# A three-block "macaron" kernel: feed-forward attention and its tail as one stage, distance tables written in parts, semaphores cleared a stage later

## What is computed

```
x = x + 0.5 * FFN(LN(x))
x = x + causal_attention(LN(x))        # 16 heads of 16, T = 1024, 32 relative distance buckets
x = x + 0.5 * FFN(LN(x))

FFN(x):                                # L = 8, N = 1024
  y1 = ln(x + mha(x), ln1)             # 4 heads; for each of 1024 positions over the L = 8
  gates = softmax(y1 @ wg); idx = argmax(gates)        # 8 experts
  loc = number of earlier tokens with the same idx; keep = loc < 1024
  h = y1 @ w1[idx] + b1[idx]           # 256 -> 1024, no nonlinearity
  z = h @ w2[idx] + b2[idx]            # 1024 -> 256
  y2 = ln(y1 + where(keep, gate * z, 0), ln2)
```

## Time and profile before

| | us |
| --- | --- |
| median of three runs | 2865.24 |
| runs | 2863.83, 2865.24, 2867.42 |
| the profiled execution's own time | 2867.24 |
| its span, first to last instruction | 2865.5 |

### The profile page before, as it was taken

One profiled execution on the slowest core, in us unless ns is written; L12 is line 12 of the kernel. 1 busy time (PEld: TensorE's weight loads), 2 busy tenths in 40 slices (PEclk: granted clock), 3 DMA queues, 4 the chain that ended last, 5 costly groups with the idle time before them and its releaser, 6 DMA issues. The chain is left out here.

```text
span 2865.5 us, 47996 instructions
## 1 busy us (share of the span) xinstructions
PE 2344.7 (82%) x15862; PEld 1425.3 (50%) x15864; DVE 2147.0 (75%) x5653; ACT 1658.5 (58%) x3995; POOL 820.4 (29%) x853
## 2 busy tenths in 40 slices
PE   3999998567739959999999999999869999983264
PEld 2666666456525523444444444444646666662243
DVE  3788888634859868898988988897447888876076
ACT  1545444313724427999999999999315445442154
POOL 1244343053544440000000000000113344331745
PEclk6999999778969978999999999999989999996587
DMA  8122120474225564454545455452341121111711
GB/s 170 30 67 67 45 67 30 162 251 138 73 88 173 170 150 89 97 111 93 109 95 113 92 103 103 99 109 45 119 154 52 45 67 54 58 38 62 210 63 68
DMA packets 244679, 281.50 MB, mean 98 GB/s; under 512 B 41808, under 2 KB 212880, under 8 KB 243808
## 3 DMA queue, kind: packets, MB, share of 16 engines
q1 hardware_dynamic: 218192, 218.81, 30.5%
q0 software_dynamic: 16384, 50.35, 5.6%
q10 hardware_dynamic: 9872, 9.45, 1.0%
HBM read 190.63 MB, written 94.16 MB: 99 GB/s over the span
## 5 line engine op out<-in xcount | busy, mean ns | idle before, releaser
L2146 DVE CUSTOM_DVE_ANT_0 banks<-banks,attn_bias 128x128 f32<-128x128 f32 (+7 forms) x1024 | 760.0, 778 | 108.4 <-PE banks L1855 82.6
L2059 ACT ACTIVATE attn_probT<-banks 128x512 f32<-128x512 f32 x1152 | 622.5, 621 | 61.6 <-PE banks L1872 51.3
L1855 PE MATMUL banks<-attn_kst,attn_qst 96*128 96x512 bf16 (+3 forms) x1536 | 421.6, 336 | 23.1 <-DMA attn_kst<-kparts 12.5
L1872 PE MATMUL banks<-attn_qst,attn_kst 99*128 99x256 bf16 (+3 forms) x2176 | 410.8, 281 | 15.2 <-ACT attn_probT L2059 7.1
L1894 PE MATMUL banks<-attn_probT,attn_vb 128*32 128x256 f32 (+3 forms) x4352 | 315.6, 400 | 7.7 <-ACT attn_probT L2059 7.2
L1872 PEld LDWEIGHTS banks<-attn_qst,attn_kst 99*128 99x128 bf16 x2176 | 187.5, 97 | 169.1 <-ACT attn_probT L2059 54.9
L2204 POOL CAST attn_lowp<-attn_lowT 128x32 bf16<-128x32 f32 x64 | 13.4, 209 | 852.3 <-DVE attn_lowT L2154 852.3
L420 PE MATMUL banks<-ffn_a_xT,winT 128*128 128x512 f32 x512 | 250.6, 612 | 6.0 <-ACT ffn_a_kT L621 2.9
L1855 PEld LDWEIGHTS banks<-attn_kst,attn_qst 96*128 96x128 bf16 x1536 | 117.4, 97 | 256.7 <-DVE attn_low L2146 158.6
L2047 ACT COPY banks<-attn_biasT 128x512 f32<-128x512 f32 x384 | 227.7, 628 | 29.9 <-DMA attn_biasT<-neardT 23.2
L883 POOL TENSOR_TENSOR ffn_a_xres<-ffn_a_xin,row_ffn_out 128x1024 f32<-128x1024 f32 x32 | 75.5, 2359 | 412.4 <-DVE ffn_a_res L764 387.2
(11 more groups left out here) (254 smaller groups left out, 4482.8 us busy)
## 6 DMA issues: line engine op xcount, KB each, us to landing
attn_qst<-qparts SPq DMA_DIRECT2D x384, 64.0 KB, 2.8
attn_kst<-kparts SPq DMA_DIRECT2D x192, 128.0 KB, 4.9
rows<-ffn_a_xb SPq DMA_DIRECT2D x32, 512.0 KB, 2.9
rows<-ffn_a_y SPq DMA_DIRECT2D x32, 512.0 KB, 3.1
ffn_t_xs<-in_L_ffn_w_dram SPq DMA_DIRECT2D x16, 1024.0 KB, 10.1
attn_biasT<-neardT SPq DMA_DIRECT2D x128, 128.0 KB, 5.1
attn_bias<-neard SPq DMA_DIRECT2D x128, 128.0 KB, 2.2
qparts<-qkv_part SPq DMA_DIRECT2D x32, 384.0 KB, 2.8
```

The costliest lines, as they stand in the source:

```text
L1855: mm = nc.tensor.matmul(score[k % 2][:, a:e], qst[0:K6, u, half, hh, ii * P:(ii + 1) * P], kst[0:K6, u, hh, a:e], start=True, stop=True)
L1872: mm = nc.tensor.matmul(tbank[t % 3][:, at:at + nb * P], kst[:, u, hh, j * P:(j + 1) * P], qst[:, u, half, hh, x:x + nb * P], start=(k == ...
L2059: nc.scalar.activation(probT[:, g % 2, i, 0:w], tbank[t % 3][:, 0:w], ACT.Exp, scale=-1.0).then_inc(s_exp, 1)
L2146: nc.vector.tensor_tensor_reduce(out=part, in0=part, in1=bias[:, hh, T - w:T], scale=1.0, scalar=BIG, op0=ALU.add, op1=ALU.min, accum_out= ...
```

## The change

The change has five parts.

1. **One stage for attention and tail.** `ffn_attention` no longer opens a stage: it returns five functions, one for each engine, which the tail's engine programs call first. Its tiles are slices that the tail lends it (`Lent`): `xin`, `xb`, `xres`, `qT`, `prob`, `res` and others from the first 7 parts of `flat`, `y1` from the eighth, `kT` from `w12`, `xT` from `xT`, `vv` from `y1` of the tail. Where the tail would write what attention still reads, an engine waits: `over_yet` for the last logits (TensorE in turn 0, VectorE, SyncE in turn 1), `stored` for the stores to `rows` (VectorE ahead of the one-hot chunks, GpSimd ahead of the gathers).
2. **Early loads.** In attention's last group SyncE issues W1[0], W1[1], W2[0] to W2[3] and b2 (turn 0) or b12 (turn 1).
3. **Order in the tail of turn 0.** TensorE: `turn_w1(0)`, `(1)` ahead of `counts`; `product(1)` and `turn_w1(3)` ahead of `inverse`; `bias_sum` one expert later; the first group's transposes ahead of the last two `bias_sum` and the marks. ScalarE: `scaled` in two pieces around `w12_out(1)` and `turned(3)`; `place(0, 0)`, `place(1, 1)` ahead of the last `w12_out`; `xT_out(0, 0)` ahead of the seeds.
4. **Tables in parts.** The two transfers in `prepare` become eight of four heads each, issued by SyncE in the first feed-forward attention in groups 2 to 9, behind that group's other transfers. `attention_core` waits for all eight.
5. **Clearing a stage later.** At a stage's end only the block's own join is left. The semaphores of a stage are cleared by GpSimd inside the next one (`clear_past`), behind its first work; those of the last stage not at all.

```diff
 class Phase
     def block(self):
-        self.callback(self._clear)
+        self.callback(self._pass)
         return self.enter_context(self.core.nc.Block())
-    def _clear(self):
-        for sem in self.sems:
-            self.core.nc.gpsimd.sem_clear(sem)
-        self.core.nc.all_engine_barrier()
+    def clear_past(self):
+        if self.core.past:
+            for sem in self.core.past.sems:
+                self.core.nc.gpsimd.sem_clear(sem)
...
 prepare, SyncE
-            for way, dst in enumerate((neard, neardT)):
-                src = bass.AP(tensor=relrow.tensor, offset=way * 3 * P, ap=[[2 * 3 * P, AH], [0, P], [1, 3 * P]])
-                sp.dma_start(bass.AP(tensor=dst.tensor, offset=1, ap=[[P * PITCH, AH], [PITCH + 1, P], [1, 3 * P]]),
-                             src).then_inc(core.tables, 16)
...
 ffn_attention, SyncE
             if not under(n, 4):
                 store(n - 4, u)
+            if n == NG - 1:
+                early_loads(sp)
+            if first and 2 <= n < 2 + len(tables):
+                sp.dma_start(*tables[n - 2]).then_inc(core.tables, 16)
...
+    def over_yet(eng):
+        eng.wait_ge(s_lgsb, NG)
+    def stored(eng, u):
+        eng.wait_ge(s_store[u], 16 * (NG // 2))
+        eng.wait_ge(s_ahead[u], 16 * (NG // 2))
...
 tail, now ffn
+        def early_loads(sp):
+            if turn == 0:
+                for e in range(2):
+                    load_w1(sp, e)
+                for e in range(4):
+                    load_w2(sp, e)
+                sp.dma_start(b12[:, :], row_bcast(d["L0_ffn_b2"].rearrange("e c -> (e c)"), NE * C)).then_inc(s_w, 16)
+            else:
+                sp.dma_start(b12[:, :], b12d).then_inc(s_w, 16)
...
 ScalarE
-                scaled()
-                for e in range(1, NE):
+                scaled(0, 2)
+                w12_out(1)
+                turned(3)
+                scaled(2, CHUNKS)
+                for e in range(2, NE):
+                    if e == NE - 1:
+                        place(0, 0)
+                        place(1, 1)
                     w12_out(e)
                     if e + 2 < NE:
                         turned(e + 2)
+                xT_out(0, 0)
+                start_seeds()
...
 TensorE
+            attend_tensor(pe)
...
-                counts()
+                over_yet(pe)
                 turn_w1(0)
-                dropped()
                 turn_w1(1)
+                counts()
+                dropped()
                 product(0)
                 turn_w1(2)
+                product(1)
+                turn_w1(3)
                 inverse()
-                for e in range(1, NE):
+                for e in range(2, NE):
                     product(e)
                     if e + 2 < NE:
                         turn_w1(e + 2)
-                    bias_sum(e - 1)
+                    bias_sum(e - 2)
+                transposes(0, 0)
+                bias_sum(NE - 2)
                 bias_sum(NE - 1)
...
 VectorE
+            attend_vector(dve)
+            over_yet(dve)
...
+            for u in range(2):
+                stored(dve, u)
             for q in range(CHUNKS):
...
 attention_qkv, GpSimd
             x_rstd(1)
+            ph.clear_past()
```

More of the change, by code:

```diff
@@ L922, in tail @@
-def tail(core, name, logits, rows, d, w12d, b12d, out, turn):
+                    pe.wait_ge(s_qsb, 2 * n)
+            elif i == 1:
+                pe.wait_ge(s_ksb, 2 * n + 1)
+            elif i == 2:
+                pe.wait_ge(s_ksb, 2 * n + 2)
+            else:
+                pe.wait_ge(s_qsb, 2 * n + 1)
+            j = QK_ORDER[i]
+            for k in range(KB):
+                mm = nc.tensor.matmul(bank[QK], core.winT[:, k, j * P:(j + 1) * P], xT[:, u, k, :],
+                                      start=(k == 0), stop=(k == KB - 1))
@@ L926, in tail, with ffn @@
+def ffn(core, name, x, rows, d, w12d, b12d, out, turn, tables):
     nc = core.nc
```

1241 lines of the change are left out of this document (627 added, 614 removed).

## The result

The changed kernel takes 2800.6 us (median of four runs, 2796.3 to 2802.7) against 2866.2 us for the kernel before in the same comparison (2863.8 to 2867.4): a ratio of 0.977, 95% interval 0.975 to 0.979. In a second comparison it took 2799.9 us, ratio 0.978 (0.974 to 0.981). The forecast was 2784.6 in a range of 2752 to 2806: the way and the range held, the point was 16 us too low.

A forecast was written before the change was run, and what follows sets the result against it. TensorE was taken to set the first attention's time, with the change touching stage ends. Terms -24.6 -12.2 -11.8 -15 -12 -5 = -80.6 on 2867.24 gave 2786.6, less 2.0 to the median: 2784.6 us, range 2752 to 2806.

The forecast's parts named there:

- Step 1: Start: with the tables gone, VectorE's first statistics come at about 33.2 us in place of 57.8; -24.6 us.
- step 4: Between stages: 186 semaphore clears and six second barriers leave the path; -15 us, with 0 to 3 lost in qkv.
- Step 2: First attention: eight table parts of 4.8 us each are covered by the x loads' lead of 21.5 us; 0.
- Step 3: Joins of attention and tail: VectorE goes on at once; -12.2 us in the first feed-forward, -11.8 in the second.
- Step 5: First tail's experts: TensorE is 9 us further on at the first gather; -12 us, bounds 0 to -30.
- The weak point named in the prediction: Nothing in the trace explains the starved stretches, such as 591 to 631 us with 15.8 us of work in 40.
- R1: First tail: gathers alone set the starved stretch's end, so the experts' lead is eaten and gives 0; 2797 us, 17%.
- Step 6: Behind the experts' marks: group 0's placing, transposes and copies come ahead, so VectorE's first sum is earlier; -5 us.
- R2: Tails: a large starved stretch (40 or 36 us) is mostly filled, some 30 us go; 2755 us, 14%.
- R3: First attention: x loads behind the table parts are late, each part costing its whole price, 38 us; 2823 us, 8%.
- R4: Attentions: ten bursts of large transfers hold engines as gathers do, up to 20.5 us each; 2990 us, 3%.
- R5: Joins: early loads not early or VectorE waits, so both save only the clears, 8 of 24 us; 2801 us, 3%.

The follow-up runs named there:

- The true undo: Changed kernel with the two whole table transfers (3 MB each, 16 heads) back in the first stage: 2826.6 us, 26.0 slower than the changed kernel.
- tables_back: Changed kernel with the eight table parts issued in the first stage ahead of the x loads, none inside the attention: 2859.8 us.
- The direct undo: Changed kernel with GpSimd clearing each stage's semaphores at that stage's end, followed by a second barrier: 2823.3 us.
- the undo: Changed kernel with TensorE's and ScalarE's orders in the tail of turn 0 as before the change: 2804.6 us.
- paced gathers: Changed kernel with GpSimd waiting, from the fourth group of gathers on, until ScalarE has placed the group three before: 2807.3 us.

## Why the prediction held, and where it was off

**Step 1, the start (-24.6).** Right: 57.78 to 33.15. The true undo costs 26.0. But step 4 had counted the first stage's 16 clears (1.2 us and a barrier) besides. The stage does begin 1.9 us earlier (x is issued at 21.69, before at 23.61), and this is lost again: the sum over the identity takes 2.20 us in place of 0.17, ending with GpSimd's first operation (25.97+2.34 = 28.31). x had landed before the preparation was over, as forecast, and just this let GpSimd begin while VectorE needed what it holds.

**Step 2, the tables (0).** The sum held, the price did not: in `tables_back` parts cost 7 us each, not 4.8, at a DMA share of only 0.26. In changed the x loads took 4.9 us in the median and 13.4 at most, so the cover of 21.5 us was large enough.

**Step 3, the joins (-12.2, -11.8).** The gaps went as forecast: 0.04 us is left of each. No run puts these joins back; that is read from the two traces. The step that failed is the sentence "VectorE goes on at once": the join had also kept VectorE's chain apart from GpSimd's last two operations. Side by side, they hold VectorE up by 1.0 and 2.2 us; the chain got 2.7 us longer in the first feed-forward and 3.1 of the 3.7 us lost in the second are the same two rows (leaving the two operations out gave 5.3 to 6.1 in both feed-forwards together). That is most of the gain that the sum promised and the kernel did not give. The Trainium skill has the rule in "SBUF — State Buffer", SBUF: two separate sides: of the engines only VectorE and GpSimd contend, for a shared port pair that one instruction holds alone and for its whole length, and a VectorE operation takes it if it has two inputs in SBUF or runs in a two-port mode. By that rule an operation of VectorE that comes second can't get through before GpSimd's ends, and the trace agrees: VectorE's, begun at 489.88 and 491.50, end at 491.58 and 493.83, GpSimd's, begun before them, at 491.03 and 493.80. The first has two inputs; the second is a copy with one, and no row shows the mode in which it ran.

**Step 4, the clears (-15).** The direct undo costs 22.7 us with the 8.1 that lay in the joins: 14.6 (on another chip, so give or take a few us). By the traces it is 12.8 without the first stage, where 13.6 were forecast. The 105 clears in qkv do delay GpSimd's first sum (7.7 us, and 6.76 idle ahead of 795.02), and the core's first load is 4.7 us nearer instead of 5.8, so up to 1 us is given back there, inside the 0 to 3 that I had named.

**Step 5, the experts (-12).** Right in size by luck, wrong in its working. The order of products and turns, which I priced, is worth less than nothing: with the old one the experts are some 4 us shorter, in each of three kernels, though the new one had TensorE a product and a turn ahead at the first gather, as forecast. The 12 us came with the joined stage in every variant (88.7 to 94.9 us from gather to mark, 103.3 before), from a cause that stays open; without them the kernel would stand near 2812, outside the range. The weak point named in the prediction was the right one: the starved stretches decide here, and a lead of 9 us on TensorE does not come out of them as 9 us. R1 was right that the lead is eaten, and wrong that the stretch then stays as it was.

**Step 6 (-5).** Right: 5.5 in the trace, 4.4 by the undo.

**The rivals.** R2: the large starved stretch of the second tail is as before (gather to last scatter 208.1 and 208.3 us). R3 and R4 fall: the first attention is 0.7 us longer, the second 0.0. R5 falls: of the joins' 24 us nothing is left ahead of the first maxima.

Of the 16 us between forecast and median, 9.6 are errors of the sum, which is what the two profiled executions differ in: 6.4 the two chains behind the joins, 2.2 the clears, and the small rest. Another 4.3 are that the profiled execution of changed was the fastest of its four, and 2.0 that I had taken off because that of before was above the median of its runs.

## What to carry to other kernels

When a barrier goes, list what it had kept apart on VectorE and GpSimd, not only the wait itself: operations that never met before now hold each other up, and moving one of them may only pass the wait on. A transfer cut along its outer dimension can use fewer DMA engines, so try a cut where it is not hidden before calling it free. And where a stretch is bound by something that the trace shows only as "issue", don't convert a lead of instructions into time.

## What the hardware showed that I had not expected

- Long rows of indirect transfers by GpSimd starve all other engines, whichever way the data goes: with 64 gathers one each 1.25 us, TensorE gets one instruction in 0.7 to 2.8 us from about 20 to 35 us after the first; with 44 scatters one each 1.28 us neither TensorE nor VectorE nor ScalarE was busy from 730 to 745 us. At about three each 5 us (paced gathers, second tail, 2630 to 2705 us) it did not happen. What resource it is stays open.
- Eight transfers of 0.77 MB over four heads held SyncE's queue for 55 us at DMA share 0.26; two of 3 MB over sixteen heads were through in some 38 us at 1.06.
- Issuing is not always free: eight issues back to back held SyncE's queue for 55 us, where they took 0.6 us each when spread over eight groups, and an engine that is held so holds the stage's end.
